# One ordered list of work for a whole two-layer transformer program, with each expert layer run in two halves

## What is computed

```
x = x + 0.5 * L0_ffn(layernorm(x))      # attention (16 heads of 8) over 512 tokens, then 8 experts, one per token
x = x + L0_attn(layernorm(x))           # causal attention
x = x + 0.5 * L0_ffn(layernorm(x))      # attention and experts again
x = x + 0.5 * L1_ffn(layernorm(x))      # dense: sum over 2 LoRA variants of top_v[k] * relu(x wi') wo'
x = x + L1_attn(layernorm(x))           # causal attention
x = x + 0.5 * L1_ffn(layernorm(x))      # dense again
# inside L0_ffn, h is the normed block input plus its attention:
hn2 = layernorm(h, ln2_g, ln2_b); logits = hn2 @ gate_w + gate_b; idx = argmax(logits)
mid = relu(hn2 @ w1[e] + b1[e]); y = mid @ w2[e] + b2[e]; out = h + y[idx]
```

## Time and profile before

| | |
|---|---|
| three runs | 1133.39, 1136.26, 1139.63 us (median 1136.26) |
| profiled execution | 1130.96 us, its span 1129.0 us |
| busy in the span | PE 80%, DVE 68%, ACT 59%, POOL 27% |
| mean granted TensorE clock | 0.897 of full |

### The profile page before, as it was taken

How to read it: one execution, slowest core, us unless ns; L and a number is a source line. 1 busy time by engine, 2 the same in 40 slices (tenths; PEclk the granted TensorE clock), 3 DMA queues, 4 the chain that set the end, 5 groups by cost and what they waited for, 6 DMA issues and landing times.

```text
span 1129.0 us, 25558 instructions
## 1 busy us (share of the span) xinstructions
PE 907.8 (80%) x9800; PEld 472.7 (42%) x9800; DVE 766.4 (68%) x1289; ACT 665.7 (59%) x1448; POOL 310.1 (27%) x573
## 2 busy tenths in 40 slices
PE   2599999953883899998999999508949579999698
PEld 1123232231881445553332322308826345555355
DVE  4789899543543887789898995424456477888355
ACT  2288888830761477777888888306712238777521
POOL 4652310115341223532413101153410122311100
PEclk8599999985895799999999999758969779999989
DMA  6112131271203221112011000012010122110000
GB/s 181 43 35 59 46 99 23 52 69 52 73 33 93 58 60 37 45 41 54 26 40 39 21 3 2 1 38 76 30 40 0 47 63 58 36 35 4 3 10 28
DMA packets 77260, 49.36 MB, mean 44 GB/s; under 512 B 22242, under 2 KB 74754, under 8 KB 77154
## 3 DMA queue, kind: packets, MB, share of 16 engines
q1 hardware_dynamic: 72024, 40.42, 14.9%
q0 software_dynamic: 2496, 5.13, 1.2%
q10 hardware_dynamic: 2634, 2.36, 0.8%
HBM read 12.72 MB, written 9.21 MB: 19 GB/s over the span
## 4 chain that ended last, share of the span: by engine, by line
PE 56%; ACT 13%; issue 11%; DVE 11%; POOL 5%; DMA 3%; ACTq 1%; SPq 1%; DVEq 0%; POOLq 0%
PE ps L601 14%; PE ps L677 13%; ACT pt L737 10%; PE ps L1394 5%; PE ps L1112 4%; PE ps L1121 4%; PE ps L633 3%; DVE negm L847 3%; DVE blockm L838 3%; POOL sorted L1331 3%; PE ps L1382 3%; PE ps L607 3%; PE ps L695 2%; PE ps L637 1%; PE ps L685 1%
## 5 line engine op out<-in xcount | busy, mean ns | idle before, releaser
L737 ACT ACTIVATE pt<-ps 128x512 f32<-128x512 f32 (+1 forms) x896 | 457.4, 566 | 132.0 <-PE ps L601 85.4
L847 DVE TENSOR_REDUCE negm<-ps 128x2 f32<-128x1024 f32 x256 | 301.6, 1220 | 28.4 <-PE ps L601 26.3
L677 PE MATMUL ps<-pt,va 128*32 128x256 f32 (+1 forms) x4352 | 273.3, 340 | 16.3 <-ACT ot L743 7.3
L838 DVE TENSOR_REDUCE blockm<-ps 128x8 f32<-128x1024 f32 (+1 forms) x192 | 195.7, 1043 | 53.3 <-PE ps L601 26.3
L601 PE MATMUL ps<-ks,qs 61*128 61x128 bf16 (+2 forms) x1536 | 175.7, 297 | 31.3 <-DMA ks<-parts 12.0
L601 PE MATMUL ps<-qs,ks 64*128 64x128 bf16 (+3 forms) x1408 | 167.5, 295 | 9.6 <-ACT pt L737 3.2
L677 PEld LDWEIGHTS ps<-pt,va 128*32 128x32 f32 x4352 | 92.0, 108 | 125.0 <-issue 74.2
L601 PEld LDWEIGHTS ps<-ks,qs 61*128 61x128 bf16 x1536 | 56.2, 97 | 186.8 <-issue 99.7
L989 POOL CAST mpart<-negm 128x16 bf16<-128x16 f32 x64 | 13.0, 204 | 331.7 <-PE ps L601 128.1
L1285 DVE COPY pt<-experts 128x1156 f32 x50 | 38.8, 776 | 70.3 <-DVE upd L1296 36.8
L601 PEld LDWEIGHTS ps<-qs,ks 64*128 64x128 bf16 x1408 | 58.1, 94 | 66.7 <-ACT pt L737 47.3
(11 more groups left out here) (161 smaller groups left out, 1121.3 us busy)
## 6 DMA issues: line engine op xcount, KB each, us to landing
qs<-parts SPq DMA_DIRECT2D x80, 128.0 KB
ks<-parts SPq DMA_DIRECT2D x65, 128.0 KB
experts<-in_L_ffn_w SPq DMA_DIRECT2D x16, 256.0 KB
pt<-sorted SPq DMA_DIRECT2D x2, 1225.5 KB, 6.7
sorted<-pad_row SPq DMA_DIRECT2D x6, 384.0 KB, 8.3
qs<-mrow SPq DMA_DIRECT2D x128, 6.0 KB
pt<-y_rows SPq DMA_DIRECT2D x8, 256.0 KB, 3.8
ks<-parts ACTq DMA_DIRECT2D x15, 128.0 KB
```

The source lines that it names most:

```text
L677: ins = pe.matmul(pv_bank[32 * j:32 * j + 32, q0:q1], va[n % 2][:, kb, 4 * g + j, 0 if odd else DH + 1:VW - DH - 1 if odd else VW], pt[:, ...
L737: a.activation(pt[:, k_ % NPT, S * s:S * s + width], b_bank(o + s)[:, 0:width], ACT.Exp).then_inc(b_free, 1)
L838: v.tensor_reduce(blockm[:, g % 2, :, t, PLACES[c_]], pair_of(ka)[:, :, 0:width].rearrange("p s (b c) -> p s b c", c=P), AX, ALU.max, nega ...
L847: v.tensor_reduce(negm[:, g % 2, :, t, c_], pair_of(ka), AX, ALU.max, negate=True).then_inc(a_free, 1)
```

## The change

The phases and their loops are gone. `schedule` writes one list for the program, three `segment` lists end to end, with all other work as jobs at positions in quads. Jobs with a position beyond the last quad stand behind the attention of that segment, in the order of their positions.

- Experts run in halves of two batches: TILES is 8, SLOTS is 8 + 7 = 15 tiles, four halves in all (60 tiles, before 46). Of each expert layer the first half's norms, logits, routing and scatter, and the second half's norm of its first batch, stand inside attention (positions from `end - 10.9`); its tiles stand from `end + 0.75`. The second half's last norm, routing and scatter stand among the first half's tiles; its tiles stand from `end + 4.5`, after `xload` at `end + 4.0`.
- The first batches of the next attention are prepared (`beginning`) among the second half's tiles, or among the dense batches.
- Dense batches 8 to 11 stand from `end + 7.75`; of the last four, 12 and 13 stand at 14.2 and 15.4 of 16 quads, 14 and 15 behind. Each batch's output is sent by itself.
- In a tile the list has: turn t, up t, down t-1, turn t+1, up t+1. The up products now share one bank of the B ring and are signalled once, after the fourth. The copy of the tile on ACT is gone; there are three weight buffers and four output buffers (two before).
- Padding for all four halves is written at position 4.0 from a zeroed tile (four transfers of 15 x 129 words per partition, 990 KB each). The turning of late weights (`flip`, `perm`) stands at 14.2 to 15.2 of the first segment.
- The values are packed at 18 words a head (41 before), filled by four DVE operations a batch in place of one.
- `keep` (POOL, the normed input kept for the residual) moves to a later position.

```diff
-AHEAD = 2
-PAD_TILES = 6
-PAD_AT = range(0, SLOTS, PAD_TILES)
 ROW = P + 1
+NRES = 3
+NWE = 3
+NY = 4
...
+NEXT = [("stats", 0, 0.0), ("rstd", 0, 0.0), ("norm", 0, 0.35), ("hT", 0, 0.5), ("q", 0, 0.65), ("qrem", 0, 0.7),
+        ("k", 0, 0.8), ("krem", 0, 0.85), ("qmid", 0, 0.9), ("kmid", 0, 1.0), ("qlo", 0, 1.0), ("klo", 0, 1.05),
+        ("stats", 1, 1.2), ("rstd", 1, 1.2), ("norm", 1, 1.5), ("v", 0, 2.0)]
+NEXT_STACK, NEXT_EVERY = 0.75, 0.05
...
+BESIDE = [("lstats", 0.35), ("lrstd", 0.35), ("xfold", 0.45), ("lnorm", 0.7), ("lT", 0.9), ("gate", 1.1)]
+ALONE = [("lstats", 0.15), ("lrstd", 0.15), ("xfold", 0.2), ("lnorm", 0.5), ("lT", 0.65), ("gate", 0.85)]
+ROUTE_BESIDE = [("pick", 1.2), ("rank", 1.35), ("place", 1.4)], 1.8, 0.2
+ROUTE_ALONE = [("pick", 0.9), ("rank", 1.15), ("place", 1.2)], 1.6, 0.16
+TILE = 0.207
+UNIT = 0.26
+def tiles_of(hm, at):
+    jobs = []
+    for t in range(SLOTS):
+        up = at + TILE * t
+        jobs += [(up - (0.35 if t < 2 else 2 * TILE - 0.03), "lay", hm, t), (up - (0.3 if t == 0 else 0.05), "tt", hm, t),
+                 (up, "up", hm, t), (up + TILE + 0.02, "dn", hm, t), (up + TILE + 0.07, "ysend", hm, t)]
+    return jobs
+def routing(hm, at, how):
+    steps, scatter, every = how
+    return [(at + after, name, hm, None) for name, after in steps] + \
+        [(at + scatter + every * j, "scatter", hm, j) for j in range(TILES)]
+def norms(l, at, how):
+    return [(at + after, name, l, None) for name, after in how if l < 8 or name not in ("xfold", "gate")]
+def dense(l, at):
+    jobs = [(at + UNIT * n, name, l, n) for n in range(FB) for name in ("fu0", "fu1")]
+    return jobs + [(at + UNIT * FB + 0.01, "fdn", l, None)]
+def beginning(n, at):
+    return [(at + after, name, n + k, None) for name, k, after in NEXT] + \
+        [(at + NEXT_STACK + NEXT_EVERY * i, "stack", n, which) for i, which in enumerate(STACK)]
...
+def schedule(causal_of, loads):
...
+    first += [(-0.9, "wflip", 0, None), (2.9, "gates", 0, None), (4.0, "pads", 0, None), (8.0, "late", 0, None), (8.6, "late", 1, None)]
+    first += [(14.2 + 0.15 * f, "flip", f, None) for f in range(FLIPS)] + [(15.2, "perm", 0, None)]
+    plan = []
+    for m, (batches, end) in enumerate((([0, 1, 2, 3], 16), ([4, 5, 6, 7, 8, 9, 10, 11], 32))):
+        jobs = first if m == 0 else [(-0.6, "yadd", 2, None), (-0.5, "yadd", 3, None)]
+        for b in range(NB):
+            jobs += norms(4 * m + b, end - 10.9 + 4 * b, BESIDE if b < NB - 1 else ALONE)
+        jobs += routing(2 * m, end - 6.9, ROUTE_BESIDE) + routing(2 * m + 1, end + 1.1, ROUTE_ALONE)
+        jobs += [(end - 0.8, "xload", 2 * m, None), (end + 4.0, "xload", 2 * m + 1, None)]
+        jobs += tiles_of(2 * m, end + 0.75) + tiles_of(2 * m + 1, end + 4.5)
+        jobs += [(end + 4.05, "yload", 4 * m + b, None) for b in range(2)] + \
+            [(end + 7.75, "yload", 4 * m + b, None) for b in (2, 3)]
+        jobs += [(end + 4.45, "yadd", 4 * m, None), (end + 4.55, "yadd", 4 * m + 1, None)]
+        if m == 0:
+            jobs += beginning(4, end + 4.6)
+        else:
+            jobs += [(end + 8.1, "yadd", 6, None), (end + 8.15, "yadd", 7, None)]
+            for b, at in enumerate((4.5, 5.4, 8.1, 9.25)):
+                jobs += norms(8 + b, end + at - 0.05, ALONE)
+                jobs += dense(8 + b, end + 7.75 + 4 * UNIT * b)
+            jobs += beginning(12, end + 9.0)
+        plan += segment(batches, causal_of, jobs)
+    end, jobs = 16, []
+    for b, at in enumerate((5.5, 9.5, 14.9, 17.5)):
+        jobs += norms(12 + b, at, BESIDE if b < NB - 1 else ALONE)
+        jobs += dense(12 + b, (14.2, 15.4, 16.9, 18.4)[b])
+        jobs += [((14.2, 15.4, 16.9, 18.4)[b] + 5 * UNIT, "send", b, None)]
+    return plan + segment([12, 13, 14, 15], causal_of, jobs)
...
+                elif name == "tt":
+                    need(pe, xs_loaded[at >= TB], 16 * (n + 1))
+                    pe.transpose(b_bank(o)[:, 0:P], sorted_rows[n % 2][:, at, 0:P], identf[:, :]).then_inc(b_full, 1)
+                elif name == "up":
+                    need(pe, b_free, at_b[("tt", n, at)] + 1)
+                    pe.wait_ge(laid, number_of(n, at) + 1)
+                    for a in range(FB):
+                        ins = pe.matmul(b_tiles(o)[:, a, :], we[:, number_of(n, at) % NWE, a * P:(a + 1) * P],
+                                        hTm[:, number_of(n, at) % 2, :], start=True, stop=True)
+                    ins.then_inc(b_full, 1)
+                elif name == "dn":
+                    need(pe, b_free, at_b[("up", n, at)] + 1)
+                    for a in range(FB):
+                        ins = pe.matmul(pair_of(ka)[:, 0, 0:P], mid_e[:, number_of(n, at) % 2, a, :],
+                                        we[:, number_of(n, at) % NWE, F + a * P:F + (a + 1) * P], start=(a == 0),
+                                        stop=(a == FB - 1))
+                    ins.then_inc(a_full, 1)
...
+                elif name == "tt":
+                    if tile_before(n, at, 2):
+                        need(a, b_full, at_b[("up", *tile_before(n, at, 2))] + 1)
+                    a.activation(hTm[:, number_of(n, at) % 2, :], b_bank(o)[:, 0:P], ACT.Identity, bias=gcol[:, 3:4],
+                                 scale=gcol[:, 2:3]).then_inc(b_free, 1)
+                elif name == "up":
+                    if tile_before(n, at, 2):
+                        need(a, a_full, at_a[("dn", *tile_before(n, at, 2))] + 1)
+                    for fb in range(FB):
+                        at_ = number_of(n, at) % NWE
+                        ins = a.activation(mid_e[:, number_of(n, at) % 2, fb, :], b_tiles(o)[:, fb, :], ACT.Relu,
+                                           bias=we[:, at_, 2 * F + fb:2 * F + fb + 1])
...
+                    for odd in range(2):
+                        half = VW * H // 2
+                        dst = va[n % 2][:, :, half * odd:half * (odd + 1)].rearrange("p k (s c) -> p k s c", c=VW)
+                        for u in range(2):
+                            c0 = 64 * u + 32 * odd
+                            ins = v.tensor_tensor(dst[:, :, 4 * u:4 * u + 4, 9 * odd:9 * odd + DH],
+                                                  a_tiles(ka)[:, :, c0:c0 + 32].rearrange("p i (j e) -> p i j e", e=DH),
+                                                  bvb[:, w["n"]:w["n"] + 1, c0:c0 + 32]
+                                                  .rearrange("p o (j e) -> p o j e", e=DH).broadcast_to([P, TB, 4, DH]),
+                                                  ALU.add)
...
+                elif name == "lay":
+                    v.wait_ge(owner_step, 3 * n + 3)
+                    need(v, w_rest, 16 * len(rest))
+                    need(v, pv_done, at_pv[final_pv(last_batch(n), 3)] + 1)
+                    if tile_before(n, at, NWE):
+                        need(v, a_free, at_a[("dn", *tile_before(n, at, NWE))] + 1)
+                    k_ = SLOTS * (n % 2) + at
+                    e = v.value_load(owner[0:1, k_:k_ + 1], min_val=0, max_val=E - 1)
+                    v.tensor_copy(we[:, number_of(n, at) % NWE, :], experts[:, bass.ds(e, 1), :]
+                                  .rearrange("p o c -> p (o c)")).then_inc(laid, 1)
+                elif name == "dn":
+                    r = number_of(n, at) % NY
+                    if tile_before(n, at, NY):
+                        need(v, y_sent[r], 16 * (number_of(n, at) // NY))
+                    v.tensor_copy(numbers_y[:, r:r + 1], sorted_rows[n % 2][:, at, P:ROW].bitcast(U32))
+                    v.tensor_tensor(ysb[:, r, :], pair_of(ka)[:, 0, 0:P],
+                                    we[:, number_of(n, at) % NWE, 2 * F + FB:WE], ALU.add).then_inc(a_free, 1)
...
+                elif name == "pads":
+                    need(sp, const_done, NCONST)
+                    for hm in range(4):
+                        sp.dma_start(d["sorted"][hm].rearrange("(t p) c -> p t c", p=P), sorted_rows[0])                            .then_inc(prefilled, 16)
...
+                elif name == "xload":
+                    if n == 0:
+                        need(sp, a_free, at_a[("flip", FLIPS - 1, None)] + 1)
+                    elif n == 2:
+                        need(sp, a_free, at_a[("dn", 0, SLOTS - 1)] + 1)
+                    else:
+                        need(sp, pv_done, at_pv[final_pv(last_batch(n), 3)] + 1)
+                    for b in (0, 1):
+                        sp.wait_ge(rows_sorted[2 * (n % 2) + b], 16 * TB * (n // 2 + 1))
+                    rows = d["sorted"][n].rearrange("(t p) c -> p t c", p=P)
+                    sp.dma_start(sorted_rows[n % 2][:, 0:TB, :], rows[:, 0:TB, :]).then_inc(xs_loaded[0], 16)
```

1087 lines of the change are left out of this document (443 added, 644 removed).

## The result

The changed kernel takes 1143.45 us in the median, the kernel before 1133.35 us: a ratio of 1.007 with a 95% interval of 1.004 to 1.010, so 0.7% slower (the ratio is that of the means of eight runs each, 1142.2 and 1134.2 us; the medians are further apart). A second set of runs of both gave 1.0058 (1.0033 to 1.0083). The forecast was 1092 us, 1050 to 1140. Both the sign and the range were wrong: a gain was forecast, and 1143 us lies above the range. The profiled execution took 1143.07 us, its span is 1141.0 us.

A forecast was written before the change was run, and what follows sets the result against it. No engine was full; the target was expert and dense gaps where PE mostly waits. Gaps save 23 and 36, attention stretches lose 18 and 10, third stretch and end save 14: 1136.3 - 45 = 1091, said as 1092 us, range 1050 to 1140.

The forecast's parts named there:

- The tile: Expert tiles: circles through ACT (2.76 us) and PE (2.81) set the period, taken as 2.85, bounds 2.07 and 3.3.
- The slow start behind a seam: Tiles of a half that follows a wait: 3 us for the clock's slow start; full clock after attention.
- First gap: Between first and second attention stretch, experts and next projections: 110 us against 132.7, 23 saved.
- Second gap: Between second and third attention stretch, experts and dense batches: 157 us against 193.0, 36 saved.
- The padding: First attention stretch: four 990 KB transfers at position 4.0 on SP's queue cost between 0 and 10 us, taken as 4.
- Norms beside attention: Attention stretches: partly hidden DVE work costs 9 us and weight turns 5 in the first; 10 lost in the second.
- Third stretch and end: Last attention stretch with norm turns and dense batches, then the end: 210 us against 223.9, 14 saved.
- Attention pays more: Rival for the attention stretches: DVE or a late m stops PE, 25 us more, 1117; chance 0.25.
- POOL blocked by DVE: Rival for scatters and outputs: each takes 1.72 us, not 0.96 to 1.3; 12 us more, 1104; chance 0.11.
- The slow clock: Rival for expert tiles: pauses of 0.4 us drop the clock to 1.2 GHz, circle about 5.0 us, 1221; chance 0.13.

The follow-up runs named there:

- e1: Changed kernel with the turn of tile t+1 placed ahead of the up products of tile t: 1113.34 us, ratio 0.9832 to the kernel before.
- e14: e10 with the turn of a tile back in its place of the changed kernel: 1110.12 us, ratio 0.9803 to the kernel before.
- e10: Changed kernel with earlier tile turn, padding parted, weight turns spread, later norm turns beside attention, dense buffer freed in quarters, new dense order: 1074.56 us, ratio 0.9479.
- e11: Changed kernel with padding in four places and turn and logits of norms beside attention 0.4 quad later: 1109.36 us, ratio 0.9801 to the kernel before.
- e21: e11 with the turn of a tile one place earlier as well: 1098.11 us, ratio 0.9687 to the kernel before.
- e5: Changed kernel with the buffer of the dense down products signalled and freed in quarters: 1135.24 us, ratio 1.0015 to the kernel before.
- e6: e1 with the second half's eight scatters together right behind the places, not between tiles: 1112.56 us, ratio 0.9797 to the kernel before.
- e15: e10 with ranking, places and scatters of the second half closer together, two scatters to a tile: 1081.38 us, ratio 0.9570 to the kernel before.

## Why the forecast was wrong

By its own steps:

- **The tile, 2.85 (2.07 to 3.3).** Right: 2.74, through the chain that the text named. Of the price of the order, 60 x (2.74 - 2.1) = 38 us, e1 recovers 27 and e14 to e10 37, but e11 to e21 only 13. That the loop's own pauses would leave the clock up was right too: it is at 1.00 wherever the tiles run at this pace.
- **The slow start behind a seam, "3 us".** Mis-sized in both gaps. The first two tiles behind each seam took 3.66 and 4.55 us at a clock of 0.50, and the clock was low in most of the first 20 us. Over 14 steps of 2.74 us (38.4) the tiles behind the seam took 14.7 us more in the first gap, where 3 and 8 were said, and 10.3 more in the second, where 3 and 2.2 were said. How much of it is the clock alone is shown once, by the 3.4 us between the two profiles of the changed kernel.
- **First gap, 110.** 115.8, in the second profile 112.2. Scatter, load and seam were nearly right (7.5 us from the last down product to the next up product, for 6.5). Besides the slow start the excess is in small waits of PE of 1.5 to 3 us that had no place in the sum: for the weight copy behind the places, for the norm of the next batch (3.05), and a stop of 1.88 us for which the profile names no releaser ("issue").
- **Second gap, 157: the step that failed most.** Tiles and seam took 112.9 where 55.7 + 48 = 104 was said, some 4 us of the excess behind the seam as above; the dense part took 67.7 where 53 was said. The sentence "the down products now come in one piece, behind the next batch's first unit, which keeps PE fed" is false. PE was fed only if the turn of batch 10 and the next batch's first norm did not stand ahead of the down products, and they did. The forecast summed PE's work (10.68 a batch, 2.2 for two turns) and did not ask of each turn whether DVE, in its own order, had got that far. e10, with the order changed and the buffer freed in quarters, gives 50.6 us, where the quarters alone (e5) gave 64.2; so the work had been priced rightly and its order had not.
- **The padding, "between 0 and 10, I take 4".** It cost some 15 us. The range was drawn from the transfer's speed and the half quad of cover of `m`; that SP itself would stand 12.5 + 5.1 us on the issue of four such transfers was not thought of. The bound was too low because only the time to landing (8.3 us) was read from the earlier trace rows, and not how long SP itself was held. The trace of the kernel before had that too, for its eight padding transfers of 320 to 384 KB:

```profile
218.36 3.30 SPq L1059 DMA_DIRECT2D sorted<-pad_row  x4
...
223.04 9.14 SPq L1059 DMA_DIRECT2D sorted<-pad_row  x4
```

- **Norms beside attention, 9 + 5 in the first stretch and 10 in the second.** Right as amounts. With the padding mended the first stretch ends at 246 to 252, against 232.2 + 18 - 4 = 246; the second is 357 to 364 against 357.
- **Third stretch and end, 210.** 215.6, 212.1 to 214.0 with the late turn. Six us too low, partly the turn of the norms (1.90 us at 1123.74, 2.50 at 1002.30).
- **The rivals.** "Attention pays more" named part of what happened, PE stopped by a late `m`, and 22 of the 57 us over the forecast lie in the two attention stretches. It stopped at 1117 because it let the padding cost 10 at most and left the dense stage as it was. "POOL blocked by DVE" did not come: scatters took 1.01 us in the mean and outputs 1.05. But POOL's queue is the bound at the seam once the tiles are quick (e6, e15). The slow clock did not come from the loop's own pauses, as that rival had it; it came behind the seams, where it did slow the tiles to 4.54 us.

Sum of the misses: 18 + 6 + 4 + 24 + 6 = 58 us over the forecast's stages. Of these the padding's 11 over its 4, the dense order's 15 and the tiles' 9 are 35 us whose places are shown; the rest is in waits of 1 to 3 us and in the low clock behind them, not shown one by one.

The forecast's own conclusion, that the new order gains once nothing stands in its way, holds for e10 (1074.6 us). With the old turn, as the forecast assumed, the runs with these waits mended give 1110, not 1092 to 1101, and why 15 us of a shortened stage come back elsewhere, as stops without a releaser and a low clock behind them, stays open.

## What to carry to other kernels

In a list that all engines walk in order, price each moved step twice: by its work, and by whether the engine that feeds it has come that far in its own list at that place; a turn that stands 0.2 quad behind its norm, or ahead of products that are ready, costs more than the turn. Spread large transfers on a queue that also carries small urgent ones. Before an edit of 5 us is believed, compare the stages that it did not touch; if they moved as much, the profile has not shown the edit. Then look in them for stops that nothing in the list explains, and at the clock behind each wait.

## What the runs showed of the hardware that was not expected

- Four transfers of 967.5 KB issued in a row by SP took 12.52 us to issue, and the next one 5.07; each alone took 0.44 to 0.60 us. In the kernel before, eight of 320 to 384 KB took 3.30 us to issue for the first four and 9.14 for the others.
- One kernel, two profiles: the granted clock in the same 10 us was 0.57 and 1.00, and in the 75 us before 0.93 and 0.86. Behind the same wait of 2.1 us the clock fell in one kernel (a pair of products 0.61 us) and stayed up in another (0.39).
- Six of nine kernels with the same list in the second stretch stood still there for 2.3 to 2.5 us on PE, with ACT and DVE idle too and no releaser in the profile; their stretches are 360.7 to 364.1 us, the others 357.2 to 358.2.
- The weight copy of 128x1156 took 858 ns in the mean (776 before, in the earlier trace rows); four value fills of 280 ns each replaced one of 684.
